# Layer 1 of a two-layer graph kernel: reciprocals of the softmax sums on ScalarE as exp(-ln(sum)), and a new place for the last scores and the second membership compare

## The reference, cut to what matters

```python
q, k, v = h @ Wq + bq, h @ Wk + bk, h @ Wv + bv      # h = relu(layernorm(x)), 4 heads of 32
alpha = einsum("ehc,ehc->eh", q[dst], k[src]) / sqrt(32)
amax = segment_max(alpha, dst)
ea = exp(alpha - amax[dst])
denom = segment_sum(ea, dst)
alpha = ea / (denom[dst] + 1e-16)
out = segment_sum(v[src] * alpha[:, :, None], dst) + (h @ Wskip + bskip)
x = x + out
```

## Time and profile before

| | |
|---|---|
| median of 3 runs | 1663.34 us (1662.32 to 1664.62) |
| the profiled execution's own time | 1664.58 us |
| its span, first to last instruction | 1662.8 us |
| mean granted TensorE clock | 0.975 |
| busy over the span: PE, DVE, ACT, POOL | 1470.4, 1347.6, 1016.5, 1083.1 us |
| layer 1, first head sums to last | 317.2 to 979.8 us |

### The profile page before, as it was taken

One profiled execution on the slowest core, in us unless ns is written; L12 is line 12 of the kernel. 1 busy time (PEld: TensorE's weight loads), 2 busy tenths in 40 slices (PEclk: granted clock), 3 DMA queues, 4 the chain that ended last, 5 costly groups with the idle time before them and its releaser, 6 DMA issues. The chain is left out here.

```text
span 1662.8 us, 34477 instructions
## 1 busy us (share of the span) xinstructions
PE 1470.4 (88%) x10545; PEld 1263.5 (76%) x10546; DVE 1347.6 (81%) x3688; ACT 1016.5 (61%) x2501; POOL 1083.1 (65%) x1202
## 2 busy tenths in 40 slices
PE   5888898699999999999999974899998999998996
PEld 4666777688888888888888863777776777777775
DVE  8879665299999999999999994677776777777675
ACT  5777888556555565656665513566665666665663
POOL 2554442577777777777777605777777777777772
PEclk9999999899999999999999996999999999999999
DMA  8899887556666666666666516677666767667672
GB/s 219 274 274 313 284 300 262 157 160 180 189 174 192 175 188 183 178 182 182 182 174 185 156 45 148 148 160 174 162 163 150 171 160 172 161 158 170 149 164 68
DMA packets 162552, 302.85 MB, mean 182 GB/s; under 512 B 104113, under 2 KB 107703, under 8 KB 157524
## 3 DMA queue, kind: packets, MB, share of 16 engines
q1 hardware_dynamic: 121503, 201.19, 41.9%
q0 software_dynamic: 40896, 99.90, 24.9%
HBM read 196.84 MB, written 104.12 MB: 181 GB/s over the span
## 5 line engine op out<-in xcount | busy, mean ns | idle before, releaser
L803 POOL DMA_INDIRECT sb_kv<-kv_rows,sb_src_all x500 | 492.9, 986 | 187.1 <-issue 131.3
L831 POOL DMA_INDIRECT sb_kv<-x_rows,sb_src_all x500 | 473.8, 948 | 209.3 <-issue 109.1
L1710 ACT ACTIVATE sb_hn<-sb_xn 100x128 f32<-100x128 f32 x500 | 240.5, 481 | 265.9 <-DMA sb_kv<-x_rows,sb_src_all 225.1
L1713 ACT ACTIVATE sb_vw<-sb_kv 128x128 f32<-128x128 f32 x500 | 239.6, 479 | 0.0
L1638 ACT ACTIVATE sb_hn<-sb_xn,sb_nstat 100x128 f32<-100x128 f32 x500 | 231.5, 495 | 0.0
L1400 DVE COPY sb_hT<-ps_b 128x400 f32<-128x400 f32 x250 | 142.2, 569 | 96.1 <-PE ps_b L2005 95.3
L1797 PE MATMUL ps_b<-sb_w,sb_memberT 128*125 128x256 f32 x800 | 201.6, 391 | 18.3 <-DVE sb_xn L921 9.2
L1660 ACT COPY sb_memberT<-ps_b 100x512 f32<-100x512 f32 x150 | 75.8, 506 | 205.7 <-PE ps_b L1885 205.7
L1797 PEld LDWEIGHTS ps_b<-sb_w,sb_memberT 128*125 128x125 f32 x800 | 146.2, 193 | 41.7 <-issue 14.7
L2005 PE MATMUL ps_b<-sb_member,sb_vw 128*128 128x100 f32 x1000 | 173.8, 278 | 0.0
L2005 PEld LDWEIGHTS ps_b<-sb_member,sb_vw 128*128 128x128 f32 x1000 | 157.4, 198 | 9.8 <-issue 9.8
(11 more groups left out here) (184 smaller groups left out, 3103.0 us busy)
## 6 DMA issues: line engine op xcount, KB each, us to landing
kv_rows<-sb_kv SPq DMA_DIRECT2D x26, 1120.0 KB
sb_xn<-x_rows SPq DMA_DIRECT2D x50, 507.8 KB
sb_xn<-in_x SPq DMA_DIRECT2D x50, 500.0 KB
out_rows<-sb_xo SPq DMA_DIRECT2D x49, 500.0 KB
x_rows<-sb_xo SPq DMA_DIRECT2D x24, 1015.6 KB
sb_kv<-in_edge_attr SPq DMA_DIRECT2D x500, 32.0 KB
sb_kv<-in_x SPq DMA_DIRECT2D x28, 560.0 KB
kv_rows<-sb_xn SPq DMA_DIRECT2D x13, 1120.0 KB
```

Of the source, the lines that this page charges most:

```text
L803: pool.indirect_dma_start(out=kvs[:, k % 4, t, :], out_offset=None, in_=kv_rows, in_offset=bass.IndirectOffsetOnAxis(ap=src_all[:, n:n + 1 ...
L831: pool.indirect_dma_start(out=xs1[:, k % 4, t, :], out_offset=None, in_=x1, in_offset=bass.IndirectOffsetOnAxis(ap=src_all[:, n:n + 1], ax ...
L1710: nc.scalar.activation(hn1[:, t, :], xn1[:, k % 4, t, 0:D], ACT.Relu, scale=xn1[:, k % 4, t, D:D + 1], bias=xn1[:, k % 4, t, D + 1:XW]).th ...
L1713: nc.scalar.activation(hs1[:, t, :], xs1[:, k % 4, t, 0:D], ACT.Relu, scale=xs1[:, k % 4, t, D:D + 1], bias=xs1[:, k % 4, t, D + 1:XW]).th ...
```

## The change

On DVE the soft steps 5 and 6 (add 1e-16, reciprocal) go, and the multiplication that gives wr becomes step 5 of now six. It waits for a new semaphore, `inverse`. On ScalarE a new function inverse_sums(k-1) computes log_tot = Ln(tot + 1e-16), with the constant in a new one-column tile `tiny`, and then rtot = Exp(-log_tot). It stands behind the exponentials and two relus, ahead of both q copies; before, copy_q 0 stood between the first relu and these two. On DVE scores(k, 2) stands ahead of the weights, the second membership compare and one statistics step ahead of weigh, and the last statistics step ahead of head_sums. On TensorE turn_member 1 and 2 move from behind turn_alpha to a place between the skips and the aggregation. GpSimd sets the new constant at the start, so the counts of const_made rise by one.

```diff
--- before.py
+++ after.py
@@ -52,7 +52,7 @@
 HALVES = ((0, 5), (5, 10))
 N_ITEM = 8
 ITEM = {"h0": 1, "h1": 2, "q0": 3, "q1": 4, "m0": 5, "q2": 6, "m1": 7, "m2": 8}
-N_SOFT = 8
+N_SOFT = 6
 
 T_DVE = (STAT_STEPS + 8 + 1 + STAT_STEPS, 5)
 T_ACT = (3, 2)
@@ -197,7 +197,7 @@
         er = sb("er", [BH, WIN])
         fsum = sb("fsum", [BH, WIN])
         tot = sb("tot", [BH, WIN])
-        tot_e = sb("tot_e", [BH, WIN])
+        log_tot = sb("log_tot", [BH, WIN])
         rtot = sb("rtot", [BH, WIN])
         wr = sb("wr", [BH, WIN])
         st = sb("st", [128, 2, 2 * B, 6])
@@ -213,6 +213,7 @@
         pstat = sb("pstat", [ROWS, PB * B, 2])
         pool_st = sb("pool_st", [ROWS, 6, 2 * B])
         minus_half = sb("minus_half", [ROWS, 2 * B])
+        tiny = sb("tiny", [BH, 1])
         src_all = sb("src_all", [128, TILES], I32)
         drel_all = sb("drel_all", [128, TILES])
         wdeg_all = sb("wdeg_all", [128, TILES])
@@ -402,6 +403,7 @@
                 self.aT = s("alpha_turned")
                 self.soft = s("softmax_step")
                 self.exp = s("exp_done")
+                self.inverse = s("inverse_sums_step")
                 self.wT = s("weights_turned")
                 self.vw = s("values_weighed")
                 self.agg = s("agg_ready")
@@ -737,7 +739,8 @@
             pool.iota(tile_row[:].rearrange("o (b t) -> o b t", t=B), pattern=[[GROUP, BATCHES], [1, B]], base=0,
                       channel_multiplier=0).then_inc(const_made, 1)
             pool.memset(minus_half[:], -0.5).then_inc(const_made, 1)
-            pool.wait_ge(const_made, 8)
+            pool.memset(tiny[:], 1e-16).then_inc(const_made, 1)
+            pool.wait_ge(const_made, 9)
             pool.affine_select(out=ident[:], in_=ident[:], compare_op=ALU.not_equal, fill=1.0, base=0,
                                pattern=[[-1, 128]], channel_multiplier=1).then_inc(const_made, 1)
 
@@ -930,7 +933,7 @@
             def search_first(n):
                 if n < TG:
                     if n == 0:
-                        dve.wait_ge(const_made, 9)
+                        dve.wait_ge(const_made, 10)
                         dve.wait_ge(heads_spread, 1)
                     ins = dve.tensor_scalar(cmp1[:, n, :], banks[6][0:ROWS, 0:EROWS], thr[:, n:n + 1], None, ALU.is_lt)
                     if n == TG - 1:
@@ -1209,6 +1212,8 @@
                     dve.wait_ge(A.seg[k % 2], 16 * (k // 2 + 1))
                 elif n == 3:
                     dve.wait_ge(A.exp, k + 1)
+                elif n == 5:
+                    dve.wait_ge(A.inverse, 2 * (k + 1))
                 else:
                     dve.wait_ge(A.soft, base + n)
                 add_row, keep_row = segk[:, k % 2, 0:WIN + 1], segk[:, k % 2, WIN + 1:SEG]
@@ -1226,10 +1231,6 @@
                 elif n == 4:
                     ins = dve.tensor_tensor_scan(tot[:, ::-1], add_row[:, 1:WIN + 1][:, ::-1], fsum[:, ::-1], -BIG,
                                                  ALU.add, ALU.max)
-                elif n == 5:
-                    ins = dve.tensor_scalar(tot_e[:], tot[:], 1e-16, None, ALU.add)
-                elif n == 6:
-                    ins = dve.reciprocal(rtot[:], tot_e[:])
                 else:
                     wait(dve, A.wT, k)
                     ins = dve.tensor_tensor(wr[:], er[:], rtot[:], ALU.mult)
@@ -1311,26 +1312,22 @@
                 if prev:
                     soft_step(k - 1, 4)
                 stats(7)
-                if prev:
-                    soft_step(k - 1, 5)
                 stats(8)
-                if prev:
-                    soft_step(k - 1, 6)
                 stats(9)
-                if prev:
-                    soft_step(k - 1, 7)
                 stats(10)
                 if this:
                     scores(k, 2)
+                if prev:
+                    soft_step(k - 1, 5)
                 stats(11)
+                if nxt:
+                    members(k + 1, 1)
+                stats(12)
                 if prev:
                     weigh(k - 1)
-                stats(12)
+                stats(13)
                 if this:
                     head_sums(k)
-                stats(13)
-                if nxt:
-                    members(k + 1, 1)
                 if prev:
                     finish(k - 1, 0)
                     finish(k - 1, 1)
@@ -1362,9 +1359,9 @@
                 finish(k - 1, 1)
                 weigh(k)
                 finish(k - 1, 2)
-                for n in range(10, STAT_STEPS):
+                for n in range(8, STAT_STEPS):
                     stats(n)
-                    if n < 13:
+                    if 10 <= n < 13:
                         x1_stats(k - 1, n - 10)
                 finish(k, 0)
                 finish(k, 1)
@@ -1611,7 +1608,7 @@
                 nc.scalar.copy(kvp(b)[:, 8:10, :],
                                banks[2 + n % 4][0:ROWS, :].rearrange("p (t c) -> p t c", t=2)).then_inc(P.kv_act, 1)
 
-            act.wait_ge(const_made, 9)
+            act.wait_ge(const_made, 10)
             nc.scalar.activation(er[0:1, 0:1], ones[0:1, 0:1], ACT.Exp)
             for b in range(PB + 1):
                 for t in range(B):
@@ -1665,6 +1662,12 @@
                 act.wait_ge(A.soft, N_SOFT * k + 3)
                 nc.scalar.activation(er[:], dl[:], ACT.Exp, scale=SCALE).then_inc(A.exp, 1)
 
+            def inverse_sums(k):
+                act.wait_ge(A.soft, N_SOFT * k + 5)
+                nc.scalar.activation(log_tot[:], tot[:], ACT.Ln, bias=tiny[:]).then_inc(A.inverse, 1)
+                act.wait_ge(A.inverse, 2 * k + 1)
+                nc.scalar.activation(rtot[:], log_tot[:], ACT.Exp, scale=-1.0).then_inc(A.inverse, 1)
+
             def relus(k, first, last):
                 for t in range(first, last):
                     if real(k):
@@ -1678,10 +1681,11 @@
                 relus(k + 2, 0, 1)
                 if real(k - 1):
                     exps(k - 1)
+                relus(k + 2, 1, 3)
+                if real(k - 1):
+                    inverse_sums(k - 1)
                 if nxt:
                     copy_q(k + 1, 0)
-                relus(k + 2, 1, 3)
-                if nxt:
                     copy_q(k + 1, 1)
                 relus(k + 2, 3, 4)
                 if nxt:
@@ -1819,7 +1823,7 @@
                                               (src_f, drel_f, cnt_f)[n][:, g, :], ident[0:ROWS, 0:ROWS])
                 ins.then_inc(idx_turned, 1)
 
-            pe.wait_ge(const_made, 9)
+            pe.wait_ge(const_made, 10)
             pe.wait_ge(w0_load, 16 * 4)
             for b in range(PB):
                 if b == 4:
@@ -1947,6 +1951,10 @@
                     turn_weights(k - 1)
                     skip(k - 1, 0)
                     skip(k - 1, 1)
+                if nxt:
+                    turn_member(k + 1, 1)
+                    turn_member(k + 1, 2)
+                if prev:
                     aggregate(k - 1, 0)
                     aggregate(k - 1, 1)
                     skip(k - 1, 2)
@@ -1954,8 +1962,6 @@
                 if this:
                     turn_alpha(k)
                 if nxt:
-                    turn_member(k + 1, 1)
-                    turn_member(k + 1, 2)
                     gather_q(k + 1, 0)
                     gather_q(k + 1, 1)
```

## The result

The changed kernel takes 1902.28 us (median of 4 runs, 1900.95 to 1904.87) against 1663.98 us for the kernel before, run beside it: ratio 1.143, 95% interval 1.1406 to 1.1454. It is 238 us slower; 1895 us had been forecast.

A forecast was written before the change was run, and what follows sets the result against it. TensorE and DVE were taken to pace each other. Steps longer by 3.21 and 2.92 us plus 2 x 1.7 of clock loss gave 9.53 a pair, times 24 = 229, +2 for last steps: 1895 us, range 1795 to 1995.

The forecast's parts named there:

- The tables: ScalarE in layer 1: two table loads a step, before Ln and the second Exp, 1.28 us each; lower bound no load.
- Rival 1: One table set serves Ln and Exp, no load in the loop: steps 13.77 and 14.4 us, 1694 us; chance 0.06.
- The chain on ScalarE: Exponentials, load, Ln, load, Exp, copy q0, then q2 (TensorE's q projection of tiles 8 and 9) at D+7.48.
- D: Start of a step's first scores on DVE, the zero from which the forecast counts its times in us.
- In order behind the loads: ScalarE works in order: q copies and memberT copies queue behind inverse_sums, so TensorE's q2 waits for copy q0.
- The late aggregation: Six member transposes ahead of the aggregation on TensorE, 0.65 us; first x1 addition on DVE at W+4.13, new wait 0.9 us.
- W: Start of the transpose of the softmax weights on TensorE, forecast at D+8.18 in a plain step.
- The clock: TensorE's pause before q2 drops its clock to 1.2 GHz for 3.4 us, losing 1.7 us a step; bounds 0 and 3.4.
- Rival 2: Table loads stand in the loop, but TensorE's clock holds: 1814 us; chance 0.08.
- Rival 3: Loads dearer, or clock low for longer, up to 1.7 us more per step: about 1975 us; chance 0.12.
- the drain: About 1380 ns per table switch on ScalarE, by the Trainium skill; would add 132 us, about 2027 us.
- Rival 4: Faster: no load, copy q0 done before TensorE wants q2, GpSimd's 12.9 us a step the bound: 1636 us; chance 0.02.

The follow-up runs named there:

- experiment 1: Changed kernel with the table set that holds both Ln and Exp loaded at the start: 1692.92 us, ratio 1.0152 to the kernel before.
- Experiments 4 and 5: Kernel before plus an unread one-element Ln and Exp pair per step: ahead of copy_q 0, 1829.08 us; behind relus 5 to 7 instead, 1668.31 us.
- experiment 2: Changed kernel with copy_q 0 ahead of inverse_sums on ScalarE, both loads kept: 1878.41 us, ratio 1.1268 to the kernel before.
- experiments 6 and 7: experiment 6, and kernel before with member transposes 1 and 2 ahead of the aggregation (1758.80 us), then also the second compare ahead of weigh (1678.75 us).
- experiment 6: Changed kernel with common table set preloaded, plus copy_q 0 ahead of inverse_sums: 1660.91 us; member transposes back behind turn_alpha: 1662.25 us; both: 1644.75 us.

## Why the prediction was right

**The tables.** The upper bound was taken, two loads a step, on a judgement, and 101 loads stand in the trace. Most of the forecast hangs on this choice, and no row of the kernel before could show it. The Trainium skill ("ScalarE: Activation LUTs", section "Table sets: the hidden batching unit") has one load for ln and then exp; this trace shows a hundred in the loop, and experiment 1 shows that the page is right about the set: it holds both, once it is asked for. Rival 1 was this case, forecast at 1694 us, 30 above the kernel before, and measured at 1692.92, 25 above it on its chip.

**The chain on ScalarE.** Ln was taken at 0.40 and is 0.401; load at D+3.55, Ln at 4.87, copy of q0 at 6.85, q2 at 7.48 were forecast. From D = 713.93 the trace has 3.48, 4.78, 6.71 and 7.32. The gaps around a load had been taken as 0.04 and are 0.01 to 0.02, and the exponentials came 0.02 sooner. The pause of TensorE was forecast as 3.5 and 4.0 us, and is 3.02 in the plain step shown and 3.50 in the statistics step.

**In order behind the loads.** Experiments 4 and 5 show it: the same loads cost 161 us ahead of the copy of q0, and nothing some 4 us later in the step. That the copy is the only thing that matters there is not so: experiment 2 gives back 24 us, since the softmax's own chain then takes over as the wait.

**The late aggregation.** W+4.13 was forecast for the first addition without the clock's part. With it the trace has 727.57 - 722.49 = 5.08. The 0.2 us for leaving the array had no row of its own; with the eight products it was put at 1.07, and the trace has 1.08 (726.49 to 727.57). DVE's wait for the aggregation was forecast as about 1 us and is 1.83 in the plain step shown, with the low clock's part in it. That the late aggregation costs time without loads or low clock is shown by experiments 6 and 7: 31 us between the set alone (1692.92) and the set with the transposes back (1662.25), and a part of the 12 us when both moves are made in the kernel before.

**The clock.** The term was mis-sized: 1.7 us a step forecast, 2.0 measured (97 us over 48 steps). One low stretch of 3.4 us was assumed. The two steps timed above have that, but others have about twice as much, and the loop has 233 us at 1.2 GHz, 4.8 us a step. The rest of the step was too large by 0.3 us (16.3 and 16.8 forecast, 16.01 and 16.50 with the clock up), so the two errors cancel in the sum: 229 us were forecast for the loop, and from the first head sums to the last the trace has 231 us more (893.5 in place of 662.7). That nearness is luck. The rest of the difference, some 7 to 9 us, lies ahead of the first and behind the last, where 2 had been forecast. Rival 2, the loads with the clock up, had 1814 us and the experiment that makes it has 1805.49.

**The rivals.** Rival 3 had a clock that stays low for longer, and some of the steps show it; what would have made the loads dearer, the drain, is not in the trace. Rival 4 (faster) had its mechanism right, the hand-over of q0's bank with no load, and needed x1's finish about 1 us sooner: the two orders of experiment 6 bring that about, and give 1644.75 us where 1636 had been worked out, 22 us below the kernel before in place of 27. The gathers of GpSimd, which the rival names as the bound, then run without a gap.

## What to carry to other kernels

Before an activation function is added inside a loop, count the table loads that its neighbours will cause, and load by hand a set that holds all of them. An engine that works in order sells its idle time only at the place where it is idle: the same two loads were free beside a wait of 4 us and cost 161 us ahead of a copy that TensorE needed. A pause of some 3 us on TensorE was charged twice here, once as the pause and once more as the clock behind it.

## What the runs showed that was not expected

The low clock took back 2.0 us for each pause of 3.0 to 3.5 us, and filling 2.6 us of the pause with idle work on TensorE saved 97 us of the 238. Moving six transposes ahead of their compare, without the compare, cost 92 us in a kernel in which DVE shows 4.5 us of waits from 330 to 980 us. And taking 1.2 us a step off DVE, the busiest engine beside TensorE, is worth 22 us of the 59 (48 times 1.23) even in the best order found. The gathers of GpSimd, 12.9 us a step where a step of the kernel before took 13.5 in the mean, leave room for 27 us at most, as rival 4 had worked out: once they run without a gap, as they do in that order, time taken off DVE can very probably buy nothing more.
